# Two half units ahead of fifteen full ones, and a cut last layer, in a gather, cross-product and tower kernel

## The reference

```
e = stack([tbl_m[ids[:, m]] for m in range(32)], axis=1)            # (1024, 32, 16)
x = e; outs = []
for W in (W0, W1, W2):                                             # (32, 32, 64), (32, 64, 64), (32, 64, 64)
    x = relu(einsum('bmd,bhd,mhk->bkd', e, x, W))                  # (1024, 64, 16)
    outs.append(sum(x, axis=2))
h = concatenate([*outs, dense_ctx], axis=1)                        # (1024, 208)
h = relu(h @ W_top1 + b_top1)                                      # 512 wide
h = relu(h @ W_top2 + b_top2)                                      # 256 wide
y = h @ W_top3                                                     # (1024, 1)
```

## Time and profile before

| what | value |
|---|---|
| median of 3 runs | 680.73 us |
| lowest and highest | 674.42 and 684.67 us |
| the profiled execution | 675.9 us |
| its span, first to last instruction | 674.0 us |
| instructions in it | 7501 |
| HBM traffic over the span | 147.61 MB read, 5.25 MB written, 227 GB/s |

### The profile page before, as it was taken

How to read it: one execution, slowest core, us unless ns; L and a number is a source line. 1 busy time by engine, 2 the same in 40 slices (tenths; PEclk the granted TensorE clock), 3 DMA queues, 4 the chain that set the end, 5 groups by cost and what they waited for, 6 DMA issues and landing times.

```text
span 674.0 us, 7501 instructions
## 1 busy us (share of the span) xinstructions
PE 572.9 (85%) x2472; PEld 191.5 (28%) x2472; DVE 558.0 (83%) x231; ACT 317.5 (47%) x1311; POOL 461.0 (68%) x353
## 2 busy tenths in 40 slices
PE   0047599989989898989898989898998989895997
PEld 0002132333323232323232323232333423231332
DVE  0039798989999999999899999999998999996400
ACT  0031447364555646454646473746456464643031
POOL 5776484977878887878697979788887873443000
PEclk9998699899999899989999999999898999997999
DMA  3296685776757576767586777777685667570000
GB/s 91 65 353 218 261 300 230 271 286 254 298 223 298 223 248 253 255 256 283 214 301 241 276 282 273 285 270 287 244 311 201 248 241 309 206 243 0 1 0 0
DMA packets 32918, 153.35 MB, mean 228 GB/s; under 512 B 11600, under 2 KB 21584, under 8 KB 24816
## 3 DMA queue, kind: packets, MB, share of 16 engines
q1 hardware_dynamic: 22656, 149.31, 57.6%
q0 software_dynamic: 8192, 2.11, 2.6%
q10 hardware_dynamic: 2032, 1.46, 0.7%
HBM read 147.61 MB, written 5.25 MB: 227 GB/s over the span
## 4 chain that ended last, share of the span: by engine, by line
PE 52%; DVE 21%; DMA 11%; issue 6%; ACT 5%; SPq 3%; POOL 2%; ACTq 0%; DVEq 0%
PE acc L484 47%; DVE prod L341 19%; DMA spread<-x_scratch 6%; DMA x_scratch<-xt 4%; ACT x L392 4%; SPq L205 3%; POOL rows L295 2%; PE x L553 2%; PE x L542 1%; DVE z L353 1%; DVE xt L331 1%; DMA first<-x_scratch 1%; PE x L559 1%; PE x L546 0%; PE acc L542 0%
## 5 line engine op out<-in xcount | busy, mean ns | idle before, releaser
L341 DVE TENSOR_TENSOR prod<-spread,x 128x4096 f32<-128x4096 f32 (+2 forms) x179 | 531.1, 3022 | 47.7 <-ACT x L392 20.4
L484 PE MATMUL acc<-prod,w 128*64 128x512 f32 x1932 | 453.7, 617 | 95.1 <-DVE prod L341 89.5
L295 POOL DMA_INDIRECT rows<-table,idx x256 | 242.7, 948 | 79.0 <-issue 70.4
L307 POOL TENSOR_TENSOR prod_pool<-spread,x_pool 128x1024 f32<-128x1024 f32 x93 | 218.1, 2374 | 84.3 <-ACT x_pool L392 84.1
L484 PEld LDWEIGHTS acc<-prod,w 128*64 128x64 f32 x1932 | 147.8, 141 | 389.5 <-issue 351.7
L392 ACT ACTIVATE x<-acc 64x512 f32<-64x512 f32 x128 | 73.0, 570 | 79.0 <-PE acc L484 77.8
L407 ACT ACTIVATE relu_out<-acc 128x512 f32<-128x512 f32 x48 | 28.7, 597 | 157.3 <-PE acc L484 156.5
L400 ACT ACTIVATE relu_out<-relu_out 128x16 f32<-128x16 f32 x480 | 95.3, 200 | 0.5
L484 PE MATMUL acc<-prod_pool,w 128*64 128x512 f32 x372 | 90.9, 592 | 0.0
L400 ACT ACTIVATION_READ_ACCUMULATOR relu_out<-relu_out 128x1 f32 x480 | 89.8, 187 | 0.0
L392 ACT ACTIVATE x_pool<-acc 64x512 f32<-64x512 f32 x128 | 75.7, 591 | 1.9
(11 more groups left out here) (20 smaller groups left out, 26.9 us busy)
## 6 DMA issues: line engine op xcount, KB each, us to landing
spread<-x_scratch SPq DMA_DIRECT2D x63, 2048.0 KB, 9.3
first<-x_scratch SPq DMA_DIRECT2D x16, 512.0 KB
rows<-table,idx POOLq DMA_INDIRECT x256
x_scratch<-xt SPq DMA_DIRECT2D x64, 48.0 KB
spread<-x_scratch SPq DMA_DIRECT2D x4, 512.0 KB, 8.2
x_scratch<-xt SPq DMA_DIRECT2D x60, 32.0 KB
w<-w ACTq DMA_DIRECT2D x2, 512.0 KB, 5.7
spread<-wt SPq DMA_DIRECT2D x2, 384.0 KB, 4.4
```

What stands on the lines that cost most here:

```text
L295: nc.gpsimd.indirect_dma_start(rows[u % 2][:, j * D:(j + 1) * D], None, table, bass.IndirectOffsetOnAxis(ap=idx[:, u, j:j + 1], axis=0)).t ...
L307: nc.gpsimd.tensor_tensor(prod_pool[:, k % POOL_SLOTS, :], tiles(u, t, 1)[:, 0, :], x[:, :], ALU.mult).then_inc(pool_ready, 1)
L341: nc.vector.tensor_tensor(prod[:, at:at + count, :], tiles(u, t, count), x[:, :].rearrange("p (a n) -> p a n", a=1).to_broadcast([P, count ...
L484: last = nc.tensor.matmul(to[K * blk:K * blk + K, :], w, moving[:, blk * BLK:(blk + 1) * BLK], start=start, stop=stop)
```

## The change

The batch becomes 17 units: two of 32 samples (units 0 and 1) and fifteen of 64. In a half unit all widths are halved: 512 columns, 8 gathers in which the partitions are four quarters of the fields times 32 samples, and a quarter of a half unit's fields is stored in 2 or 3 DMAs of 32 rows of 512 bytes, 10 in all (for unit 0, five each on SP and ACT). Layers 2 and 3 of unit 0 and layer 2 of unit 1 have no tiles on POOL. The transpose of unit 1 comes right after layer 1 of unit 0, that of unit 2 after the first step of layer 3 of unit 0. The groups of unit 0 after the first are issued without a wait between them.

At the end, layer 3 of unit 15 is cut after its second step: layer 2 of unit 16 is put between the halves on DVE, PE, ACT and POOL. For it x2 of the last unit is put where x0 was, and its copy for POOL where that of x1 was; layer 3 of unit 16 uses the accumulator of its own layer 2.

Ids come in two loads on SP, laid out by the host, with the starts of the tables in them. ACT runs a small activation before its first stores. In the tower, layer 1 runs on 480 columns for the full units; each half unit's 32 samples have three matmuls of 128 rows for the two partition halves of z together, and one of 16 rows for the dense inputs. The result is stored in four DMAs. A wait of PE on the accumulator's last reader is now written out for every stage (`bank_of`, `BANKS`).

The diff, cut to its core:

```diff
-UNITS = 16
-S = B // UNITS
+S = 64
...
-F = 2
-J = M // F
+J = 16
...
+HALVES = 2
+UNITS = HALVES + (B - HALVES * S // 2) // S
+LAST = UNITS - 1
+FULL = (UNITS - HALVES) * S // 2
+COLS = FULL + HALVES * S // 2
...
+def width(u):
+    return N // 2 if half(u) else N
+def fields(u):
+    return J // 2 if half(u) else J
+def copies(u, f):
+    return 3 if f * fields(u) < J else 2
+def stores(u):
+    return sum(copies(u, f) for f in range(4)) if half(u) else 8
+def z_at(u):
+    return FULL + u * S // 2 if half(u) else (u - HALVES) * S // 2
...
-    return () if (layer, u) == (2, 0) else (5, 6, 7)
+    return () if (layer, u) in ((2, 0), (3, 0), (2, 1)) else (5, 6, 7)
...
+    second = 1 if pool_tiles(layer, u) else 4
     if layer == 2:
-        return (0, 2), (2, 2), (4, 4 if u == 0 else 1), (8, 4), (12, 2), (14, 2)
-    return (0, 4), (4, 1), (8, 4), (12, 4)
+        return (0, 2), (2, 2), (4, second), (8, 4), (12, 2), (14, 2)
+    return (0, 4), (4, second), (8, 4), (12, 4)
...
+CUT = 2
+CUT_ORDER = ([("step", 0), ("step", 1), ("pool", 0), ("pool", 1), ("pool", 2)], [("step", 2), ("step", 3)])
+def sequence():
+    def every(layer, u):
+        return [(layer, u, i) for i in range(len(steps_of(layer, u)))]
+    yield from every(1, 0)
+    for u in range(LAST):
+        yield from every(2, u)
+        yield from every(1, u + 1)
+        if u + 1 < LAST:
+            yield from every(3, u)
+    yield from every(3, LAST - 1)[:CUT]
+    yield from every(2, LAST)
+    yield from every(3, LAST - 1)[CUT:]
+    yield from every(3, LAST)
...
+        ids0_sb = sb("ids0_sb", [P, 2, J // 2], i32)
+        ids_sb = sb("ids_sb", [P, J // 2 + (UNITS - HALVES + 1) * J], i32)
+        idx = sb("idx", [P, J + (UNITS - HALVES) * J], i32)
...
+        def store_half(engine, u, f):
+            for copy in range(copies(u, f)):
+                to = scratch(u, J // 2 * f + M * copy)
+                to = bass.AP(tensor=to.tensor, offset=to.offset, ap=[[N // 8, 4], [N // 2, J // 2], [1, N // 8]])
+                engine.dma_start(to, xt[u % 2][32 * f:32 * f + 32, 0:N // 8]).then_inc(scratch_in[u % 2], 16)
...
-                src = scratch[u, t, :]
-                src = bass.AP(tensor=src.tensor, offset=src.offset, ap=[[N, RUN], [8 * N, STEP], [N, count], [1, N]])
-                sp.dma_start(tiles(u, t, count), src).then_inc(landed, 16)
+                src, n = scratch(u, t), width(u)
+                src = bass.AP(tensor=src.tensor, offset=src.offset, ap=[[n, RUN], [8 * n, STEP], [1, count * n]])
+                sp.dma_start(tiles(u, t, count).rearrange("p t n -> p (t n)"), src).then_inc(landed, 16)
...
-            for f in range(F):
-                sp.dma_start(ids_sb[64 * f:64 * f + 64, 0:1, :],
-                             ids.rearrange("(u s) (f j) -> f s u j", s=S, f=F)[f, :, 0:1, :]).then_inc(ids_in, 16)
-            for f in range(F):
-                sp.dma_start(ids_sb[64 * f:64 * f + 64, 1:UNITS, :],
-                             ids.rearrange("(u s) (f j) -> f s u j", s=S, f=F)[f, :, 1:UNITS, :]).then_inc(ids_rest_in, 16)
+            sp.dma_start(ids0_sb[:, :, :], ids0).then_inc(ids0_in, 16)
+            sp.dma_start(ids_sb[:, :], ids).then_inc(ids_in, 16)
             sp.wait_ge(turned, 1)
-            store(sp, 0, 0)
+            for f in range(0, 4, 2):
+                store_half(sp, 0, f)
...
+            for g in range(1, GROUPS):
+                load_group(0, g)
+            for u in range(LAST):
                 sp.wait_ge(turned, u + 2)
-                for f in range(F):
-                    store(sp, u + 1, f)
+                if half(u + 1):
+                    for f in range(4):
+                        store_half(sp, u + 1, f)
+                else:
+                    store(sp, u + 1)
...
-                sp.dma_start(out.rearrange("(u g b) o -> g o u b", g=2, u=UNITS)[g],
-                             y[:, g, :].rearrange("p (u b) -> p u b", u=UNITS)).then_inc(stored, 16)
-            sp.wait_ge(stored, 32)
+                sp.dma_start(out[HALVES * S // 2:B, :].rearrange("(u g b) o -> g o u b", g=2, b=S // 2)[g],
+                             y[:, g, 0:FULL].rearrange("p (u b) -> p u b", b=S // 2)).then_inc(stored, 16)
+                sp.dma_start(out[g * S // 2:(g + 1) * S // 2, :].rearrange("b o -> o b"),
+                             y[:, g, FULL:BLK]).then_inc(stored, 16)
+            sp.wait_ge(stored, 64)
...
-                for j in range(J)[part]:
+                at0 = u * J // 2 if half(u) else HALVES * J // 2 + (u - HALVES) * J
+                for j in range(fields(u))[part]:
...
+            products(LAST - 1, 2)
+            products(LAST - 1, 3)
+            products(LAST, 2)
+            products(LAST, 3)
...
+                n = fields(u) * D
+                e = D // 4 if half(u) else D // 2
+                nc.vector.transpose(xt[u % 2][:, 0:n].rearrange("p (b e) -> p e b", e=e),
+                                    rows[u % 2][:, 0:n].rearrange("p (j e c) -> p e c j", e=e, c=D // e)).then_inc(turned, 1)
...
+            turn(1)
+            for u in range(LAST):
                 dve.wait_ge(x_ready[0], u + 1)
                 for i in range(len(steps_of(2, u))):
                     multiply(2, u, i, x1)
-                    if u == 0 and i == 2:
-                        turn(1)
                 if u == 0:
                     sum_d(0, 0)
-                if u + 1 < UNITS:
-                    layer_1(u + 1)
+                layer_1(u + 1)
                 dve.wait_ge(x_ready[1], u + 1)
-                for i in range(len(steps_of(3, u))):
-                    if i == 3 and u + 2 < UNITS:
-                        turn(u + 2)
-                    multiply(3, u, i, x2)
-                    if i == 2:
-                        sum_d(u, 1)
-                if u + 1 < UNITS:
+                if u + 1 < LAST:
+                    for i in range(len(steps_of(3, u))):
+                        if i == (1 if u == 0 else 3) and u + 2 < UNITS:
+                            turn(u + 2)
+                        multiply(3, u, i, x2)
+                        if i == 2:
+                            sum_d(u, 1)
                     sum_d(u + 1, 0)
-            sum_d(UNITS - 1, 2)
+            for i in range(CUT):
+                multiply(3, LAST - 1, i, x2)
+            sum_d(LAST - 1, 1)
+            dve.wait_ge(x_ready[0], LAST + 1)
+            for i in range(len(steps_of(2, LAST))):
+                multiply(2, LAST, i, x1)
+            sum_d(LAST, 0)
+            for i in range(CUT, len(steps_of(3, LAST - 1))):
+                multiply(3, LAST - 1, i, x2)
+            dve.wait_ge(x_ready[1], LAST + 1)
+            for i in range(len(steps_of(3, LAST))):
+                multiply(3, LAST, i, x2_of(LAST))
+                if i == 1:
+                    sum_d(LAST, 1)
+            sum_d(LAST, 2)
...
+            act.wait_ge(consts_in, 48)
+            nc.scalar.activation(warm[:, :], w_sq[0:1, 0:1], ACT.Relu)
             act.wait_ge(turned, 1)
-            store(act, 0, 1)
+            for f in range(1, 4, 2):
+                store_half(act, 0, f)
...
+            after_2(LAST)
+            after_3(LAST - 1)
+            sum_3(LAST - 1)
+            after_3(LAST)
...
+            done = layer(LAST - 1, 3, CUT_ORDER[0])
+            layer(LAST, 2, order_of(2, LAST))
+            layer(LAST - 1, 3, CUT_ORDER[1], done)
+            layer(LAST, 3, order_of(3, LAST))
...
-                        nc.tensor.matmul(to_h1(t, g), w_top1[own, l, t * P:(t + 1) * P], z[own, l, :],
-                                         start=l == 0, stop=False)
+                        nc.tensor.matmul(to_h1(t, g)[:, 0:FULL], w_top1[own, l, t * P:(t + 1) * P],
+                                         z[own, l, 0:FULL], start=l == 0, stop=False)
                 for g in range(2):
                     own = slice(64 * g, 64 * g + D)
-                    nc.tensor.matmul(to_h1(t, g), w_dense[own, t * P:(t + 1) * P], dense[own, :],
+                    nc.tensor.matmul(to_h1(t, g)[:, 0:FULL], w_dense[own, t * P:(t + 1) * P], dense[own, 0:FULL],
+                                     start=False, stop=True)
+                for g in range(HALVES):
+                    for l in range(3):
+                        nc.tensor.matmul(to_h1(t, g)[:, FULL:BLK], w_top1[:, l, t * P:(t + 1) * P],
+                                         z[:, l, z_at(g):z_at(g) + S // 2], start=l == 0, stop=False)
+                    own = slice(64 * g, 64 * g + D)
+                    nc.tensor.matmul(to_h1(t, g)[:, FULL:BLK], w_dense[own, t * P:(t + 1) * P], dense[own, FULL:BLK],
                                      start=False, stop=True).then_inc(h1_mm, 1)
```

More of the change, by code:

```diff
@@ new lines, in places, with pool_places @@
+def places():
+    out, owner, at, made = {}, [0] * RING, 0, 0
+    for number, (layer, u, i) in enumerate(sequence()):
+        count = steps_of(layer, u)[i][1]
+        if at + count > RING:
+            at = 0
```

(25 more changed lines are left out.)

266 lines of the change are left out of this document (132 added, 134 removed).

## The result

The changed kernel takes 685.12 us in the median of 20 runs (679.47 to 693.03) against 680.13 for the kernel before on the same chip: a ratio of 1.0084, interval 1.0053 to 1.0114. So it is slower, by 0.8%, where 1.1% faster was forecast. (Every ratio here compares fast runs with fast runs, so it can differ a little from the ratio of the medians.) Its profiled execution took 683.49 us with a span of 681.3, 7.3 longer than before.

| stage (profiled executions) | forecast | measured | row |
|---|---|---|---|
| start, to layer 2 of the first full unit | -11.6 | 93.52 to 90.16: -3.4 | DVE |
| thirteen units between | 0 | 35.95 to 36.07 each: +1.5 | DVE |
| tail, to the end of the last reduce | -5.0 | 75.57 to 71.32: -4.3 | DVE |
| tower, first layer | +8.0 | 16.27 to 25.62: +9.4 | PE |
| tower, second layer | 0 | 13.9 to 16.7: +2.8 | PE |

What follows compares the result with a forecast made beforehand. PE and DVE, both above 80% busy, were taken as nearly full, leaving gains at the start and end: 675.9 - 11.6 - 5.0 + 8.0 + 1.2 = 668.5 us profiled, 673 on the median; range 664 to 684.

Steps and rivals of the forecast that it cites:

- The start: Time to layer 2 of the first full unit: 93.52 to 81.9, 11.6 us gained (range 4 to 16).
- layer 1 of unit 2 waits 0.4 for its group: In the start, DVE's wait for unit 2's group load before its layer 1: 0.4 us.
- about 1.2: In the start, layer 1 of unit 1 waits about 1.2 us for stores' landing, first load and group load.
- 3.2 for the reduce: In the start, unit 2's layer 1 reduce on DVE waits 3.2 us for PE and ACT (1.1 to 5.5).
- The tower: First tower layer: 64 narrow matmul pairs at 0.15 us, less 1.6 saved; 8.0 us lost (5.4 to 26).
- The tail: Cut layer 3 of unit 15 covers DVE's 5.14 us pause and slow matmuls; 1.6 load wait; 5.0 gained (2.0 to 6.6).
- The output: At the end, four stores instead of two: 1.2 us lost.
- The middle: Fourteen full units between start and tail, left at 35.9 us each: no gain or loss.
- (b): Rival: half units don't pay, PE's clock falls at short layers' handovers; start gives about 1, total 684 us; chance 0.15.
- (a): Rival: both ends give all they have, narrow matmuls run at weight loads' pace; 666 us on the median; chance 0.20.
- (c): Rival: narrow tower matmuls cost what wide ones do, 0.43 us each; +25.9 in the tower, 691 us; chance 0.05.
- (d): Rival: the tail's cut does nothing, 5.14 us wait stays for the fourth group; 678 us; chance 0.60 together with forecast.

Runs made afterwards that it cites:

- e10: Changed kernel with wide stores, half units' sums folded ahead of the last reduce, unit 1's stores ahead of unit 0's third and fourth group loads: 671.56 us, ratio 0.984.
- e12: e10 with unit 2's stores issued on SP right behind its transpose, ahead of unit 1's last group load: 668.25 us, ratio 0.9806 to the kernel before.
- e1: Changed kernel with the half units' sums added beforehand on ACT and DVE, tower on 512 columns without narrow matmuls: 682.12 us, ratio 1.002.
- e2: Changed kernel with 4 stores of 32 rows for a half unit in place of 10 with 4 outermost: 683.67 us, ratio 0.9969.
- e3: Changed kernel with the last three layers in the old order, the cut undone: 693.47 us, ratio 1.0174 to the kernel before.
- e6: Changed kernel with the tower's narrow matmuls of all four tiles moved behind the wide ones: 685.82 us, ratio 1.0108 to the kernel before.
- e4: The kernel before with only the cut of the last layers added, no half units: 676.4 us, ratio 0.9903.
- e8: e5 with 22 and 26 added matmuls keeping PE busy ahead of layer 1 of units 1 and 2: 679.86 us, ratio 1.0012.
- e5: Changed kernel with both the early addition of e1 and the wide stores of e2: 676.7 us, ratio 0.9968 to the kernel before.
- e7: e5 with the stores of units 1 and 2 issued by ScalarE instead of SP: 680.43 us, ratio 0.9991 to the kernel before.

## Why the prediction was wrong

- **The start failed, in the waits.** Up to layer 2 of unit 0 it held (31.4 forecast, 32.41 measured), in part by luck: the first transpose came 0.8 earlier than reckoned (14.94 for 15.7) and the way from it took 1.7 longer. The step that failed is "layer 1 of unit 2 waits 0.4 for its group" (3.81), and with it the "about 1.2" for layer 1 of unit 1 (5.06), the waits that the prediction itself named as its sign of being wrong; 3.2 for the reduce was near (2.75 + 1.23). I had checked that POOL's gathers of unit 2 are done by 46, but had not followed the chain behind them: transpose at 51.2, SP held to 54.58 by unit 1's loads, landing, first tile, group load. The row of before at 72.91 showed the same samples' load as a wait already, and I had not read it. e10 and e12 show that this chain, and not the wait before unit 1, sets the start: 8.2 of the 15.0 us between the sum, 668.5, and the profiled 683.49.
- **The tower failed, in the clock.** Its term was 64 x 0.15 - 1.6 = 8.0; the pairs took 0.14, so the price was right. The step that failed is that this term held nothing for the clock, which fell to half in and behind them: 2.2 in the fourth tile, 2.8 in the second layer, and 4.2 more than forecast for the stage in all. That narrow matmuls are the cause, e1 shows with the towers of e2, e3 and e6; when the clock falls among them isn't known, and e3's tower lost 3.4 more.
- **The tail held** in its number: 4.3 gained for 5.0 forecast, the group load 1.99 late where I took 1.6. In its mechanism one step was wrong, at no cost: PE did stand still, for 2.40 up to 606.28, and its clock was 0.50 from 608 to 610, where I had no pause and no slow matmuls; the last reduce waits 4.39 (5.82 before), as it does in e4, where PE paused for 0.77 only. e3 and e4 show the cut's gain from both sides (6.5 and 4.5 in the tail). **The output held.**
- **The middle** was taken as 0 and came to 1.5. In the ten profiles whose thirteen units can all be read it runs from 35.9 (e10) to 36.5 a unit (e4), so 0.12 between two of them is no more than profiles of like kernels differ by.
- **Of the rivals**, (b) came nearest in the number (684) and in the start (it gave 1, measured 3.4), but not by its mechanism: the clock did fall at the half units' pauses, and e8 took that away for next to nothing. Nor does its "about 1" follow from its own figures: 31.4 + 64 is 95.4, later than 93.52. (a) fell with the waits of the start, (c) with 0.14 a pair, (d) with the 6.60 of e3, which the cut takes away.

## What to carry over

A start made shorter is worth what the next unit's data allow: follow the second unit's chain through every queue before the first one's gain is booked, and look in the old trace whether that unit already waits. Narrow matmuls on the path can cost more than their own time, as the clock may fall in or behind them; adding the halves beforehand cost nothing once it stood in a pause. And an added VectorE instruction with two SBUF operands is best put where GpSimd isn't multiplying.

## What the runs showed of the chip that was not expected

- The granted clock fell to 0.50 while the profile shows TensorE busy 100%, at 32-column matmuls that had begun at 650.89 (0.57 in the window from 654, e6); it was 1.00 again in the window from 668, with 512-column ones running since 664.13. In e2 and e3 it fell at the wide matmuls behind the first tile's narrow ones, 5.9 us into the tower.
- A VectorE addition of 64x96 took 6.1 to 6.9 us beside GpSimd's multiplies and 0.24 to 0.30 without them.
- With the loads of three groups (3 MB) ahead of four small stores, the load that waits for the stores went out 7 us behind them, whether SP (e5) or ScalarE (e7) had issued them; with two of the three behind the stores, 2.2 (e10).
- A four-row store took 0.64 to issue on SP, a 32-row one with more bytes 0.47 (1.87 for 4), a 16-row one 0.49 (3.92 for 8).
